# State space stage of a decoder kernel: x sigmoid(x) taken as h + h tanh(h), with one more scalar pass and GpSimd products

## The chip, the cores and the metric

One core of one Trainium2 chip runs the whole kernel. The metric is the device time of one execution in microseconds (us); the median of several executions stands for a kernel.

## What is computed

The kernel is a decoder of four layers over x of 64 x 64 x 128. The change is in one of its twelve stages, the state space layer of the third layer. Its reference, cut to what matters:

```python
xr = x @ w_in + b_in
xc, res = jnp.split(xr, 2, axis=-1)
u = jax.nn.silu(_causal_conv(xc, w_conv, b_conv))      # 4 taps along time
x_dbl = u @ w_x
dt, B, C = jnp.split(x_dbl, [DTR, DTR + N], axis=-1)   # N = 16
delta = jax.nn.softplus(dt @ w_dt)
deltaA = jnp.exp(delta[..., None] * A)
deltaBu = delta[..., None] * B[:, :, None, :] * u[..., None]
# h = a * h + bu along time, for each of the 16 states
y = jnp.einsum('bldn,bln->bld', hs, C) + u * D
return y * jax.nn.silu(res) @ w_out
```

silu(x) is x sigmoid(x). It is taken twice, of the convolved half (u) and of the gate half (res).

## The kernel before, in words

`state_space` (from line 2404) works on 8 groups of 512 positions (g = 0 to 7, `NG`), with the 256 inner channels in two halves of 128 partitions (c = 0, 1). Within a group it loops over the 16 states; step m = 16 g + k is state k of group g. Each engine has its own program in order, written out by hand, and they meet by semaphores.

Per step and half: the scalar engine makes the decay exp(A delta) (`decay`, L2697) into one of three PSUM banks in turn; GpSimd makes the product of du and the row of B (`inputs`, L2762) into one of two buffers per half; the vector engine runs the scan (`scan`, L2851) and multiplies by the row of C (`contribute`, L2859); TensorE lays out the row of C (`c_row`, L2527) and adds up over k (`accumulate`, L2544). I write scan(k,c) for the scan of state k, half c. The program of the vector engine in step k is scan(k,0), contribute(k-1,1), scan(k,1), contribute(k,0). In step k the scalar engine makes decay(k+1,0) and decay(k+1,1), and GpSimd the inputs of k+1. decay(k,c) may start when the scan three before it in order is done, since there are three banks; an input of k may start when the scan of k-2 in the same half is done.

Into these steps is woven the preparation of the next group, g+1. On the scalar engine: `raw` (L2627) takes the convolution out of PSUM with its bias in k = 1 and 3 (it waits for TensorE's four-tap convolution, L2501) and the gate half in k = 5 and 6 (L2491); in k = 6, behind those, `silu_u` (L2636) and `silu_res` (L2643), each one pass of 128 x 1024 with the Silu table; in k = 7 `copy_dt` and `copy_bc` (L2649, L2657) of the projection by w_x (`projected`, L2510), in k = 8 `high_part` (L2666), for which the vector engine waits in `below_high` (L2836) in k = 9, between contribute(8,1) and scan(9,1); in k = 9 and 10 `step_size` (L2674, L2675, and an Exp, L2681), in k = 11 `softplus` (L2685, Ln). On the vector engine in k = 7: layer norm statistics of group g+2 (L660, L666) and `residual` of group g-1 (L2869), after which TensorE may reuse the bank for `projected`. On GpSimd: `gated` (L2777, the product with the gate of the group before) in k = 2 and 3, a reciprocal root in k = 8, splitting of B and C in k = 9 to 11, `step_size` and `stepped_input` (L2767, L2772) in k = 12 to 15. SyncE fetches the rows of B by DMA, four steps ahead.

Group 0 has no group before it under which to hide, so its preparation (the head of the stage) is one chain through the engines.

The scalar engine holds one set of function tables at a time; where a pass needs another, the compiled program has an ACT_TABLE_LOAD ahead of it, shown with the line of that pass.

Of the kernel before, what the change touches and what calls it, by code (L numbers as in the profile page):

```python
# [18 lines left out]
ALU = mybir.AluOpType  # L19
ACT = mybir.ActivationFunctionType  # L20
# [6 lines left out]
GT = NT * P  # L27
# [612 lines left out]
NG = 8  # L640
# [1763 lines left out]
def state_space(nc, e, W):  # L2404
# [6 lines left out]
    use = ssm_order()  # L2411
    names = PN_SEMS + ("zeroed misc_mm misc_cp taps_done u_done res_done hi_done parts_own bc_parts relu_done sp_own sp_done "
                       "nb_raw nb_done dl_done du_done c_mm a_done bu_done hs_done hc_done acc_mm yo_done yr_done "
                       "h_mm h_cp raw_done low_done b_out b_in0 b_in1 b_in2 b_in3")
    with block_of(nc, "state_space", names) as (block, s):
        room = Room(e.arena)
        u_t = room.take(3 * 2 * GT)
# [17 lines left out]
        at, cbank, acc = (lambda i: e.bank((0, 1, 4)[i % 3])), (lambda m: e.bank(2 + m % 2)), (lambda c: e.bank(5 + c))  # L2435
        ln = PipedNorm(e, s, room, e.X, lambda g: xn, 1e-5)
        nb = room.pair(NT)

        @block.sync
        def _(sp):  # L2440
# [144 lines left out]
        def _(a):  # L2585
# [6 lines left out]
            def told(g):  # L2592
                return s["misc_cp"] if g else s["h_cp"]
# [22 lines left out]
            def raw(step, g):  # L2616
                c = int(step[-1]) % 2
                have(step, g)
                if step[0] == "c":
                    if g >= 1:  # L2620
                        a.wait_ge(s["u_done"], 2 * g)
                    out, bias = raw_u[:, c * GT:(c + 1) * GT], W("b_conv")[:, c:c + 1]
                else:
                    if g >= 2:
                        a.wait_ge(s["yr_done"], 2 * (g - 1))
                    out, bias = res(g, c), W("b_in")[:, 2 + c:3 + c]
                a.activation(out, bank(step, g), ACT.Identity, bias=bias).then_inc(told(g), 1)  # L2627

            def silu_u(g):
                if g == 0:  # L2630
                    a.wait_ge(s["h_cp"], HEAD["cv1"] + 1)
                else:
                    a.wait_ge(s["misc_cp"], use["cv1", g] + 1)
                if g >= 3:
                    a.wait_ge(s["misc_mm"], use["y", g - 3] + 1)
                a.activation(u_b(g), raw_u, ACT.Silu).then_inc(s["u_done"], 2)  # L2636

            def silu_res(g):
                if g == 0:
                    a.wait_ge(s["h_cp"], HEAD["m3"] + 1)  # L2640
                else:
                    a.wait_ge(s["misc_cp"], use["m3", g] + 1)
                a.activation(res_b(g), res_b(g), ACT.Silu).then_inc(s["res_done"], 1)  # L2643

            def copy_dt(g):
                have("db", g)
# [75 lines left out]
            for m in range(M):  # L2722
                g, k = m // N, m % N
                decay(m + 1, 0)
                decay(m + 1, 1)
                if g + 1 < NG:
                    if k in (1, 3):
                        raw(("cv0", "cv1")[k // 2], g + 1)
                    if k in (5, 6):
                        raw(("m2", "m3")[k - 5], g + 1)  # L2730
                    if k == 6:
                        silu_u(g + 1)
                        silu_res(g + 1)
                    if k == 7:
                        copy_dt(g + 1)
                        copy_bc(g + 1)
                    if k == 8:
                        high_part(g + 1)
                    if k in (9, 10):
                        step_size(k - 9, g + 1)  # L2740
                    if k == 11:
                        softplus(g + 1)
                if g + 2 < NG:
                    if k == 12:
                        scale(g + 2)
                    if k == 13:
                        copy_ln(g + 2)
                    if k in (14, 15):
                        channels(k - 14, g + 2)

        @block.gpsimd
        def _(q):
# [16 lines left out]
            def stepped_input(g, c):  # L2769
                q.wait_ge(s["dl_done"], 2 * g + c + 1)  # L2770
                q.wait_ge(s["u_done"], 2 * (g + 1))
                q.tensor_tensor(du(g, c), delta(g, c), u(g, c), ALU.mult).then_inc(s["du_done"], 1)  # L2772

            def gated(g, c):
                q.wait_ge(s["res_done"], g + 1)
                q.wait_ge(s["yo_done"], 2 * g + c + 1)
                q.tensor_tensor(u(g, c), u(g, c), res(g, c), ALU.mult).then_inc(s["yr_done"], 1)  # L2777

# [26 lines left out]
            for m in range(M):  # L2805
# [4 lines left out]
                inputs(m + 1)  # L2810
                if k in (2, 3) and g >= 1:
                    gated(g - 1, k - 2)
                if g + 1 < NG:
                    if k == 9:
                        middle(g + 1, "bu_done", 2 * (m + 2))
# [15 lines left out]
        def _(v):  # L2831
            def below_high(g):
                v.wait_ge(s["hi_done"], g + 1)
                if g >= 1:
                    v.wait_ge(s["bc_parts"], g)
                v.tensor_tensor(rest, raw_bc, bcp(g)[0:32, :], ALU.subtract).then_inc(s["low_done"], 1)  # L2836

            def first_step_size():
                v.wait_ge(s["relu_done"], 2)
# [31 lines left out]
            for i in range(3):  # L2871
                v.memset(tiles(at(i), NB)[:, :, 0:1], 0.0)
            v.memset(xp_all, 0.0).then_inc(s["zeroed"], 1)
            ln.stats(v, 0)
            ln.stats(v, 1)
            for c in range(2):
                for i in range(4):
                    ins = v.tensor_scalar(taps(c, i), e.ident, W("w_conv")[:, 4 * c + i:4 * c + i + 1], None, ALU.mult)
            ins.then_inc(s["taps_done"], 1)
            below_high(0)  # L2880
            first_step_size()
            for m in range(M):
# [1096 lines left out]
```

## Time and profile before

| | |
|---|---|
| median of 3 executions | 3262.33 us (3258.98 to 3262.79) |
| profiled execution, device time | 3257.66 us |
| profiled execution, span of the trace | 3255.9 us |
| state space stage in the trace | about 1490 to 2036 us |
| busy over the span | PE 82%, PEld 58%, DVE 59%, ACT 39%, POOL 44% |

PE is TensorE's matmuls and PEld its weight loads, DVE the vector engine, ACT the scalar engine, POOL GpSimd, SP SyncE. Lines such as L2851 are lines of the kernel before. An idle time with "<-" behind it was ended by what stands there. Where work of several engines overlaps, the time of the stage is set by the engine that never waits, and only what makes that one wait costs time.

### The profile page before, as it was taken

How to read it: one execution, taken by the hardware profiler on the slowest of the kernel's cores; microseconds unless marked ns; L12 is line 12 of the kernel's file. 1: busy time of each engine (PE TensorE's matmuls, PEld its weight loads, DVE VectorE, ACT ScalarE, POOL GpSimd, SP SyncE). 2: the span in 40 equal slices, each digit the busy share in tenths (PEclk: the TensorE clock that was granted, in tenths of full speed). 3: DMA queues.
4: the chain of work that ended last, by engine and by line, in shares of the span. 5: the costliest groups of instructions: out<-in, count | busy, mean ns of one | idle time of the engine just before them, and what ended most of it. 6: DMA issues, size and time to landing. Idle time of an engine off the chain costs nothing. (4 is left out here: it accounts for less than half of the span.)

```text
span 3255.9 us, 72437 instructions
## 1 busy us (share of the span) xinstructions
PE 2659.4 (82%) x28079; PEld 1876.5 (58%) x28079; DVE 1921.4 (59%) x4181; ACT 1277.8 (39%) x2160; POOL 1429.6 (44%) x1573
## 2 busy tenths in 40 slices
PE   7988849989999898885888886866769999982493
PEld 4655539967777565572333332534449898862493
DVE  4757752146777466533999999345657666544123
ACT  3533434411111144123666563432326656640253
POOL 5646532231222263543888877433541111115555
PEclk9989959989999899796999999877779999995797
DMA  7000016600000100152212221000000000001375
GB/s 243 2 1 2 2 49 176 171 29 3 3 3 3 42 15 8 41 168 67 69 66 70 71 66 52 1 1 1 2 8 9 5 9 5 2 2 56 112 229 156
DMA packets 116739, 164.30 MB, mean 50 GB/s; under 512 B 33264, under 2 KB 78704, under 8 KB 115952
## 3 DMA queue, kind: packets, MB, share of 16 engines
q1 hardware_dynamic: 101456, 143.13, 14.5%
q0 software_dynamic: 7168, 14.78, 1.3%
q8 instruction: 226, 3.70, 0.5%
q10 hardware_dynamic: 7776, 1.77, 0.3%
q14 instruction: 113, 0.93, 0.1%
HBM read 137.20 MB, written 25.62 MB: 50 GB/s over the span
## 5 line engine op out<-in xcount | busy, mean ns | idle before, releaser
L674 POOL TENSOR_SCALAR arena<-arena 128x4 f32<-128x4 f32 x120 | 27.6, 230 | 950.9 <-DVE arena L666 700.4
L2762 POOL TENSOR_TENSOR arena<-arena 128x512 f32<-128x512 f32 x256 | 321.3, 1271 | 71.4 <-DVE arena L2851 62.7
L2851 DVE TENSOR_TENSOR_SCAN arena<-ps,arena 128x512 f32<-128x512 f32 x256 | 313.0, 1223 | 31.3 <-ACT ps L2697 28.7
L2544 PE MATMUL ps<-arena,const_w 128*128 128x512 f32 x512 | 275.4, 623 | 16.8 <-DVE arena L2859 15.6
L163 PEld LDWEIGHTS ps<-L_attn_w,arena 128*128 128x128 f32 x1984 | 241.5, 193 | 59.6 <-issue 38.9
L163 PE MATMUL ps<-L_attn_w,arena 128*128 128x128 f32 x1984 | 258.8, 281 | 11.9 <-ACT arena L2627 4.7
L2697 ACT ACTIVATE ps<-arena,aneg 128x504 f32<-128x504 f32 x256 | 166.5, 677 | 61.6 <-DVE arena L2851 60.9
L1827 PE MATMUL ps<-arena,L_attn_w 128*128 128x512 f32 x384 | 184.5, 617 | 0.9 <-ACT arena L755 0.9
L1895 ACT ACTIVATE arena<-ps,L_attn_w 128x512 f32<-128x512 f32 x64 | 44.0, 687 | 332.7 <-PE ps L1827 332.7
L2859 DVE TENSOR_TENSOR arena<-arena,ps 128x512 f32<-128x512 f32 x256 | 170.8, 668 | 0.0
L435 ACT ACTIVATE arena<-ps 128x1024 f32<-128x1024 f32 x96 | 98.4, 1025 | 151.0 <-PE ps L337 151.0
L2544 PEld LDWEIGHTS ps<-arena,const_w 128*128 128x128 f32 x512 | 93.8, 195 | 106.8 <-DVE arena L2859 68.4
L429 ACT ACTIVATE arena<-arena 128x1024 f32<-128x1024 f32 x96 | 101.3, 1055 | 100.1 <-DVE arena L562 100.0
L491 POOL TENSOR_TENSOR arena<-arena,const_w 128x1024 f32<-128x1024 f32 x64 | 121.0, 1898 | 43.3 <-PE ps L325 35.9
L2291 DVE TENSOR_REDUCE arena<-arena 128x8 f32<-128x512 f32 x128 | 87.2, 681 | 84.1 <-ACT arena L2178 83.9
L163 PE MATMUL ps<-L_attn_w,ct_all 128*128 128x128 f32 x1024 | 131.0, 280 | 2.1 <-DVE arena L2307 2.0
L1125 DVE SCALAR_TENSOR_TENSOR arena<-ps,arena 128x64 f32 x108 | 30.7, 284 | 170.0 <-PE ps L925 160.7
L676 POOL TENSOR_TENSOR arena<-arena,mhalf 128x4 f32<-128x4 f32 x120 | 125.2, 1044 | 10.0
L700 POOL TENSOR_SCALAR arena<-x_all,arena 128x128 f32<-128x128 f32 x160 | 125.3, 796 | 7.4 <-POOL arena L676 6.4
L163 PEld LDWEIGHTS ps<-L_attn_w,ct_all 128*128 128x128 f32 x1024 | 123.0, 194 | 8.8 <-DVE arena L2307 3.8
L351 PEld LDWEIGHTS ps<-arena 128*64 128x64 f32 x3072 | 100.1, 139 | 42.0 <-issue 20.7
L337 PE MATMUL ps<-const_w,arena 128*128 128x128 f32 x768 | 105.9, 282 | 21.3 <-ACT arena L429 21.3
(460 smaller groups left out, 6389.8 us busy)
## 6 DMA issues: line engine op xcount, KB each, us to landing
arena<-b_rows SPq DMA_DIRECT2D x128, 256.0 KB, 3.1
arena<-zone_w SPq DMA_DIRECT2D x54, 512.0 KB
arena<-pair_w SPq DMA_DIRECT2D x40, 578.0 KB
arena<-rt SPq DMA_DIRECT2D x24, 384.0 KB
pair_in<-pair_free SPq DMA_DIRECT2D x1, 5200.0 KB, 37.8
arena<-pair_in SPq DMA_DIRECT2D x40, 130.0 KB
arena<-ctx SPq DMA_DIRECT2D x16, 256.0 KB, 3.5
arena<-pair_out SPq DMA_DIRECT2D x16, 256.0 KB, 5.2
```

What stands on the lines that cost most here:

```text
L163: ins = pe.matmul(out, src[:, j * P:(j + 1) * P], w, start=(i == 0), stop=(bias is None and i == len(chunks) - 1))
L337: ins = pe.transpose(e.bank(0, 2)[:, hp * P:(hp + 1) * P], sc(i)[:, hp * P:(hp + 1) * P], e.ident)
L429: a.activation(sc(i), sc(i), ACT.Exp, scale=scale).then_inc(s["p_ready"], 1)
L491: p_.tensor_tensor(kbd(i), repeat(k(g)[:, j * P:(j + 1) * P], HH), spread(e.hmask8, P), ALU.mult).then_inc(s["kbd_done"], 1)
L676: q.tensor_tensor(rs[:, NT:2 * NT], rs[:, 0:NT], self.e.mhalf[:, 0:NT], ALU.pow).then_inc(self.rstd_s, 1)
L700: q.tensor_scalar(self.dst(g)[:, j * self.step:j * self.step + D], self.src(g)[:, j * D:(j + 1) * D], mv[:, 2 * j:2 * j + 1], rs[:, NT + j ...
L1827: pe.matmul(e.bank(i), W(w)[:, col], xnT(g), start=True, stop=True).then_inc(s["qkg_mm"], 1)
L2544: pe.matmul(acc(c), e.ident, hc(m, c), start=(k == 0), stop=(k == N - 1)).then_inc(s["acc_mm"], 1)
L2697: a.activation(tiles(at(i), NB)[:, :, 1:S], tiles(delta(g, c), NB)[:, :, 1:S], ACT.Exp, scale=e.aneg[:, c * N + k:c * N + k + 1]).then_inc ...
L2762: q.tensor_tensor(bu(m, c), du(g, c), bs(m), ALU.mult).then_inc(s["bu_done"], 1)
L2851: v.tensor_tensor_scan(hs(m, c), at(2 * m + c), bu(m, c), 0.0, ALU.mult, ALU.add).then_inc(s["hs_done"], 1)
L2859: v.tensor_tensor(hc(m, c), hs(m, c), cbank(m), ALU.mult).then_inc(s["hc_done"], 1)
```

## The change

silu(x) = h + h tanh(h) with h = x/2. `raw` stores h in place of x (scale 0.5 and halved biases `half_b`, made by two small vector instructions in the head). `silu_u` becomes a Tanh pass and moves from k = 6 to k = 3, behind the `raw` of the second convolved half; the new `one_more` adds 1 to it in k = 4, behind the two decays; GpSimd multiplies by h in k = 4 and 5, one half in each. `silu_res` becomes a Tanh pass into a new tile `gate_t` and moves to k = 8, ahead of `high_part`; its `one_more` stands in k = 14, and GpSimd multiplies in k = 6 and 7 of the next group. In group 0 the vector engine does (tanh + 1) h for both in one instruction each (`first_silu`).

```diff
@@ ACT, raw @@
-                    out, bias = raw_u[:, c * GT:(c + 1) * GT], W("b_conv")[:, c:c + 1]
+                    out, bias = raw_u[:, c * GT:(c + 1) * GT], half_b[:, c:c + 1]
-                    out, bias = res(g, c), W("b_in")[:, 2 + c:3 + c]
-                a.activation(out, bank(step, g), ACT.Identity, bias=bias).then_inc(told(g), 1)
+                    out, bias = res(g, c), half_b[:, 2 + c:3 + c]
+                if g == 0:
+                    a.wait_ge(s["half_done"], 1)
+                a.activation(out, bank(step, g), ACT.Identity, bias=bias, scale=0.5).then_inc(told(g), 1)
@@ ACT, silu_u and silu_res @@
-                a.activation(u_b(g), raw_u, ACT.Silu).then_inc(s["u_done"], 2)
+                a.activation(u_b(g), raw_u, ACT.Tanh).then_inc(s["tu_done"], 1)
-                a.activation(res_b(g), res_b(g), ACT.Silu).then_inc(s["res_done"], 1)
+                if g >= 1:
+                    a.wait_ge(s["res_done"], 2 * g)
+                a.activation(gate_t, res_b(g), ACT.Tanh).then_inc(s["tr_done"], 1)
+
+            def one_more(t, sem, g):
+                a.wait_ge(s[sem], 2 * g)
+                a.activation(t, t, ACT.Identity, bias=1.0).then_inc(s[sem], 1)
@@ ACT, the loop over m, for the group g + 1 @@
-                    if k == 6:
+                    if k == 3:
                         silu_u(g + 1)
+                    if k == 4:
+                        one_more(u_b(g + 1), "tu_done", g + 1)
+                    if k == 8:
                         silu_res(g + 1)
+                    if k == 14:
+                        one_more(gate_t, "tr_done", g + 1)
@@ POOL @@
+            def silu_u(g, c):
+                q.wait_ge(s["tu_done"], 2 * g + 1)
+                q.tensor_tensor(u(g, c), u(g, c), raw_u[:, c * GT:(c + 1) * GT], ALU.mult).then_inc(s["u_done"], 1)
+
+            def silu_res(g, c):
+                q.wait_ge(s["tr_done"], 2 * g + 1)
+                q.tensor_tensor(res(g, c), gate_t[:, c * GT:(c + 1) * GT], res(g, c), ALU.mult).then_inc(s["res_done"], 1)
+
             def gated(g, c):
-                q.wait_ge(s["res_done"], g + 1)
+                q.wait_ge(s["res_done"], 2 * g + c + 1)
@@ POOL, the loop over m, behind inputs(m + 1) @@
+                if k in (4, 5) and g + 1 < NG:
+                    silu_u(g + 1, k - 4)
+                if k in (6, 7) and g >= 1:
+                    silu_res(g, k - 6)
@@ DVE, the head @@
+            def first_silu():
+                v.wait_ge(s["tu_done"], 1)
+                v.scalar_tensor_tensor(out=u_b(0), in0=u_b(0), scalar=1.0, in1=raw_u, op0=ALU.add,
+                                       op1=ALU.mult).then_inc(s["u_done"], 2)
+                v.wait_ge(s["tr_done"], 1)
+                v.scalar_tensor_tensor(out=res_b(0), in0=gate_t, scalar=1.0, in1=res_b(0), op0=ALU.add,
+                                       op1=ALU.mult).then_inc(s["res_done"], 2)
+            for i, part in enumerate((W("b_conv"), W("b_in")[:, 2:4])):
+                ins = v.tensor_scalar(half_b[:, 2 * i:2 * i + 2], part, 0.5, None, ALU.mult)
+            ins.then_inc(s["half_done"], 1)
```

## Rows read from the trace of the kernel before

**Rows 1.** Busy time by window; columns: window, its us, each engine, PEclk, DMA share, GB/s
```profile
1650.00:1710.00 60.00, 49.88 (x130) 19.91 (x130) 58.39 (x76) 37.23 (x57) 50.09 (x45) 1.00 0.21 67
```
**Rows 2.** Groups of ACT, 1490 to 2050: count, busy us, mean ns, idle before
```profile
L2697 ACT ACT_TABLE_LOAD x15 | 19.2, 1283 | 1.7 <-DVE arena L2841 1.4
...
L2636 ACT ACT_TABLE_LOAD x7 | 9.0, 1283 | 0.1
```
**Rows 3.** Groups of DVE, 1490 to 2050
```profile
L2851 DVE TENSOR_TENSOR_SCAN arena<-ps,arena 128x512 f32<-128x512 f32 x256 | 313.0, 1223 | 31.3 <-ACT ps L2697 28.7 <-POOL arena L2762 1.5
```
**Rows 4.** Timeline of DVE: start, us, what, [idle before it], three scans behind Silu
```profile
1567.84 1.22 DVE L2851 TENSOR_TENSOR_SCAN arena<-ps,arena 128x512 f32<-128x512 f32 x1 [1.98 <-ACT ps L2697]
...
1630.28 1.22 DVE L2851 TENSOR_TENSOR_SCAN arena<-ps,arena 128x512 f32<-128x512 f32 x1 [1.40 <-ACT ps L2697]
...
1940.11 1.22 DVE L2851 TENSOR_TENSOR_SCAN arena<-ps,arena 128x512 f32<-128x512 f32 x1 [2.51 <-ACT ps L2697]
```
**Rows 5.** Timeline, steps 4 to 7 of group 1
```profile
1612.21 3.74 POOL L2762 TENSOR_TENSOR arena<-arena 128x512 f32<-128x512 f32 x3
...
1615.29 0.69 ACT L2627 ACTIVATE arena<-ps,L_attn_w 128x512 f32<-128x512 f32 x1 [3.46 <-PE ps L2501]
...
1615.87 1.89 ACT L2697 ACTIVATE ps<-arena,aneg 128x504 f32<-128x504 f32 x3
...
1616.74 1.22 DVE L2851 TENSOR_TENSOR_SCAN arena<-ps,arena 128x512 f32<-128x512 f32 x1
...
1620.16 1.22 DVE L2851 TENSOR_TENSOR_SCAN arena<-ps,arena 128x512 f32<-128x512 f32 x1
...
1623.58 1.23 DVE L2851 TENSOR_TENSOR_SCAN arena<-ps,arena 128x512 f32<-128x512 f32 x1
```
**Rows 6.** Timeline, step 5 of group 0
```profile
1553.59 2.65 ACT L2697 ACTIVATE ps<-arena,aneg 128x504 f32<-128x504 f32 x4
...
1554.30 1.22 DVE L2851 TENSOR_TENSOR_SCAN arena<-ps,arena 128x512 f32<-128x512 f32 x1 [0.37 <-ACT ps L2697]
```
**Rows 7.** Timeline, steps 7 to 9 of group 1
```profile
1628.21 0.66 DVE L2869 TENSOR_TENSOR x_all<-ps,x_all 128x512 f32<-128x512 f32 x1
...
1628.93 1.96 PE L2510 MATMUL ps<-arena,L_attn_w 128*96 128x512 f32 x4
...
1630.92 0.59 ACT L2649 ACTIVATE arena<-ps 64x512 f32<-64x512 f32 x1
...
1632.02 1.26 ACT L2697 ACTIVATE ps<-arena,aneg 128x504 f32<-128x504 f32 x2
...
1633.31 0.63 ACT L2666 ACTIVATE bcp<-arena 32x512 bf16<-32x512 f32 x1
...
1633.71 1.22 DVE L2851 TENSOR_TENSOR_SCAN arena<-ps,arena 128x512 f32<-128x512 f32 x1
...
1635.54 0.68 DVE L2836 TENSOR_TENSOR arena<-arena,bcp 32x512 f32<-32x512 f32 x1
```
**Rows 8.** Groups of POOL, 1490 to 2050
```profile
L2777 POOL TENSOR_TENSOR arena<-arena 128x512 f32<-128x512 f32 x16 | 20.3, 1271 | 8.2 <-DVE arena L2864 8.2
```
**Rows 9.** Timeline of the head
```profile
1505.02 1.06 ACT L2643 ACTIVATE arena<-arena 128x1024 f32<-128x1024 f32 x1
1507.73 0.69 ACT L2627 ACTIVATE arena<-ps,L_attn_w 128x512 f32<-128x512 f32 x1 [1.66 <-PE ps L2501]
...
1521.81 1.28 ACT L2681 ACT_TABLE_LOAD   x1
...
1526.66 1.22 DVE L2841 TENSOR_TENSOR arena<-arena 128x1024 f32<-128x1024 f32 x1 [7.84 <-ACT arena L2685]
```
**Rows 10.** Groups of DVE, 1490 to 2050: a vector instruction of few columns
```profile
L3141 DVE TENSOR_SCALAR arena<-L_xattn_w 128x1 f32<-128x1 f32 x1 | 0.2, 156 | 1.0 <-PEq L55 1.0
```
**Rows 11.** Groups of ACT, 2050 to 2170, the next stage (Tanh L3062, Exp L3040)
```profile
L3062 ACT ACTIVATE arena<-ps,arena 128x512 f32<-128x512 f32 x8 | 5.5, 687 | 19.1 <-PE ps L2987 19.1
L3040 ACT ACTIVATE arena<-arena 128x512 f32<-128x512 f32 x8 | 5.0, 620 | 0.0
```

More of the change, by code:

```diff
@@ L2413, in state_space @@
                        "nb_raw nb_done dl_done du_done c_mm a_done bu_done hs_done hc_done acc_mm yo_done yr_done "
-                       "h_mm h_cp raw_done low_done b_out b_in0 b_in1 b_in2 b_in3")
+                       "h_mm h_cp raw_done low_done tu_done tr_done half_done b_out b_in0 b_in1 b_in2 b_in3")
     with block_of(nc, "state_space", names) as (block, s):
@@ L2437, in state_space @@
         nb = room.pair(NT)
+        gate_t, half_b = room.take(2 * GT), room.take(4)
         @block.sync
@@ L2879, in _ @@
             ins.then_inc(s["taps_done"], 1)
+            first_silu()
             below_high(0)
```

## The prediction

> **What bounds the kernel now.** The page gives no answer for this stage, so I read in this order: busy time by window, groups by line, the vector engine in order of time, then one group of all engines. By window the stage belongs to the vector engine: 58.4 of 60 us, against 50.1 on GpSimd, 49.9 on TensorE and 37.2 on the scalar engine [rows 1]. Its scans wait 28.7 us for decays of the scalar engine and 1.5 us for GpSimd [rows 3]; nothing else holds it up between its head and its end. So a microsecond in which the scan waits is a microsecond of the kernel, and everything else lies under the scans. The reader is to see that GpSimd has 10 us of slack in 60, and that the slack is worth only what the order of its program lets it use.
>
> In order of time one scan starts 1.71 us after the last (1616.74 to 1620.16 is two) [rows 5]. Behind the Silu passes of each group it sits idle: 1.98 us in group 0, 1.40 in groups 1 to 5 (five alike, one shown), 2.51 in group 6 [rows 4]. Normally a successor overlaps the end of its forerunner by 0.09 us (a raw of 0.69 at 1615.29, the next at 1615.87, is 0.58 apart and overlaps 0.11), so counted from start to start the losses are 2.07, 1.49 and 2.60.
>
> **Removed: the table changes.** Seven loads stand ahead of Silu and seven of the fifteen at the decays are its way back, 14 x 1.283 = 18.0 us of scalar time [rows 2]. In the next stage eight Exp and eight Tanh passes alternate without any load [rows 11], so the two functions share a set, and I take it that Tanh among decays needs none. What goes on the path is only the scan's waits: 2.07 + 5 x 1.49 + 2.60 = 12.1 us. A gain of the full 18.0 isn't to be had, since the scan never waited for that much. The Trainium skill (ScalarE: Activation LUTs, What ACT_TABLE_LOAD costs) puts a switch to another set at 2.66 us, drain included, which would make 37 us of scalar time. The row has the load alone, 1.283 us with 0.1 idle ahead of it over seven, so the trace does not show the drain.
>
> **Added first: Tanh in k = 3.** TensorE hands over the second convolution late: the raw pass starts at 1615.29 after 3.46 us of waiting, decay(5,0) follows at 1615.87 and ends at about 1616.56, and scan(5,0) starts at 1616.74 [rows 5]. There is 0.14 us of room. Tanh must wait for the end of raw (1615.98), starts at about 1616.05, lasts 1.06 as other 128 x 1024 passes do [rows 9], and decay(5,0) can start 0.96 later, 1617.01, ends 1617.69, and the scan starts at 1617.73 instead of 1616.74: +0.99. In group 0 the decay has no room at all (decay 1553.59, scan 1554.30 after a wait of 0.37 [rows 6]); there it is 1553.01 + 0.69 + 0.07 + 0.96, decay from 1554.7, scan at 1555.44: +1.14.
>
> **Added second: GpSimd's wait for one_more.** This is the dear one. In k = 4 GpSimd has ended inputs(5) at about 1615 (three from 1612.21, the third of which is already the first of k = 6 [rows 5]); now silu_u(0) stands ahead of that third one and waits for one_more. one_more follows decay(5,0) and decay(5,1): 1617.64 + 0.63 = 1618.27, done 1619.33. Queued behind this wait are the inputs of k = 6. GpSimd's products come every 1.25 us (3.74 for three) [rows 5] and last 1.27 [rows 8]. silu_u(0) at 1619.40, input (6,0) at 1620.65, done 1621.92. scan(6,0) is due at 1620.16 + 0.99 = 1621.15 and starts at 1621.95: +0.80. Input (6,1), silu_u(1), input (7,0) follow at 1621.90, 1623.15, 1624.40, done 1625.67. scan(7,0) is due at 1623.58 + 1.79 = 1625.37, starts 1625.70: +0.33. After that the statistics and residual of k = 7 give GpSimd room for silu_res (2.5 us in k = 6 and 7). Sum here 2.12 in groups 1 to 6, 2.27 in group 0.
>
> **Added third: the gate's Tanh ahead of high_part.** With the stall behind Silu gone, the next late thing is the projection. TensorE can't start it before residual is done (1628.87), starts 1628.93, and copy_dt starts at 1630.92 [rows 7]. Decay(9,0) follows 1.10 later, 1632.02, ends 1632.70. scan(8,0) would be due at 1628.79, scan(9,0) at 1632.22, and starts at 1632.74: +0.52. Until now this hid in the Silu stall. Then decay(9,1), and Tanh in front of high_part: high_part ends 0.63 + 0.63 + 0.96 + 0.63 = 2.85 after decay(9,0) starts, 2.90 with its signal. below_high was due 1.83 after scan(9,0) (1633.71 to 1635.54 [rows 7]), that is 0.72 + 1.83 = 2.55 after decay(9,0): +0.35. In group 0 there is no residual and nothing of this; in group 6 no statistics cover it (about 1.2 us less vector work in k = 7), part of which TensorE's order takes, so I put 1.1 for 0.52.
>
> **Added where it costs nothing:** one_more in k = 14 (the scalar engine waits for TensorE there), silu_res on GpSimd in k = 6 and 7, the other decays, and SyncE's rows of B, fetched four steps ahead. If the cover of silu_res were gone, each group would pay up to 2.5 us more.
>
> **The head.** Its Tanh of the gate may need a load of 1.28, which with the pass ends at 1507.4, ahead of the next raw at 1507.73: hidden. The load ahead of the first Exp (1521.81, on the chain) then goes, -1.28. The projection now waits for first_silu, priced by a 128 x 1024 product of two SBUF tiles, 1.22 [rows 9], plus 0.05 of signal: +1.27; as a fused form it may take 1.5. Two instructions of few columns ahead of the statistics, between 0 and 0.156 each [rows 10]: +0.2. Head: +0.2, between -0.2 and, if the first Exp keeps its load, +1.8.
>
> **The sum.** Group 0: 2.27 - 2.07 = +0.20. Groups 1 to 5: 2.12 + 0.52 + 0.35 - 1.49 = +1.50 each, +7.5. Group 6: 2.12 + 1.1 + 0.35 - 2.60 = +0.97. Head +0.2. Total +8.9: 3257.7 of the profiled execution becomes 3266.6. That one is 4.7 below the median, so beside the median 3262.3 I say 3271.2. Bounds: the terms at their smallest (0.9, 0.6, 0.1, 0, 0.1) leave +0.2 a group and +1 in all; at their largest (1.1, 0.9, 0.4, 0.7, 0.5) +2.1 a group, with the head's upper end +16. So 3263 to 3278 for this case.
>
> **The rivals.** (1) *Faster: the waits are gone and nothing takes their place.* That holds if raw comes 0.99 us earlier at k = 3, the point from which Tanh fits ahead of decay(5,0), and one_more with it and 0.8 earlier still, so that input (6,0) is ready in time. Then -12.1 + 0.2: 3250.4. For it: 10 us of slack on GpSimd, 23 on the scalar engine [rows 1]. Against: 0.14 us of room at 1616.74, in every group. The Trainium skill's rule (ScalarE: Activation LUTs, Table sets: the hidden batching unit) to batch passes by set rather than by function speaks for this rival. Chance 0.13. (2) *Only the scalar terms count, GpSimd's are covered:* its wait for one_more costs the scans nothing if inputs (6,0) is not late. 0.99 + 0.52 + 0.35 - 1.49 = +0.37 a group, some +2.5 in all, 3265. This asks for one_more 0.8 us sooner against the scans than I have it, as if GpSimd needed no 0.07 to start and one_more didn't stand behind decay(5,1). Against: both stand in the code. Chance 0.22. (3) *The tables aren't shared in this stage:* then each Tanh brings two loads, 5.1 us a group on decays with no room, 7 x 5.1 + 9 = +45: 3307. Against it [rows 11]. Chance 0.04. (4) GpSimd falls further behind than I have it, so that its root and splitting in k = 8 to 11 come late too: up to 2 us a group more, 3285. Chance 0.06. Forecast 0.55.
>
> **How the numbers follow.** About 0.2%, 6.5 us, is what a measurement of this kernel tells from no change, so same is 3255.8 to 3268.8. Slower: 0.48 of the forecast's 0.55, 0.02 of case 2, cases 3 and 4: 0.58. Same: the rest of the forecast, most of case 2 and 0.01 of case 1: 0.28. Faster 0.14. The range leaves out most of case 1 and all of 3 and 4's far part: 3257 to 3281.
>
> **What would show it.** ACT loads fall from 31 in the stage to 17; Those at L2697 are eight, behind Ln, and L2636 has none. The wait of scans for the Tanh'd decays appears at scan(5,0) as 0.9 us, for POOL at scan(6,0) and (7,0) as 0.7 and 0.25, for ACT at scan(9,0), and below_high waits 0.3. GpSimd sits 4.7 us ahead of silu_u(0) in each group. If scans wait for POOL nowhere, my second term is wrong; if scan(5,0) doesn't wait, the first; if loads remain at L2697 beyond those behind Ln, case 3.

## The result, and the profile after

| | before | after |
|---|---|---|
| median of 7 runs each, us | 3262.3 (3258.53 to 3262.95) | 3273.19 (3271.89 to 3290.77) |
| ratio of the two, 95% interval | | 1.0047 (1.003 to 1.0064) |
| profiled execution, its own time, us | 3257.7 | 3290.77 |
| its span, us | 3255.9 | 3289.0 |
| state space stage in the trace, us | 544.58 | 561.90 |
| stage start to first scan, us | 40.68 | 42.77 |
| scan(5,0) of one group to that of the next, groups 1 to 5, us | 61.97 | 63.76 (65.5 and 65.8 in two of them) |
| ACT table loads in the stage | 31 | 17 |

The change costs 10.9 us at the medians; 8.9 was predicted. 14.5 us of what the profiled execution of after takes more lie ahead of the stage (it begins at 1504.62 and not at 1490.07), where nothing was changed, so I compare the stage and not the spans.

The groups of the scalar engine and of the vector engine in the stage, 1480 to 2060 (columns as in [rows 2]: count, busy us, mean ns, idle before and what ended it), answer to [rows 2] and [rows 3]:

```profile
L2694 ACT ACT_TABLE_LOAD x8 | 10.3, 1283 | 0.1
L2706 ACT ACT_TABLE_LOAD x8 | 10.3, 1283 | 1.6 <-DVE arena L2875 1.4
L2690 ACT ACT_TABLE_LOAD x1 | 1.3, 1283 | 0.0
...
L2885 DVE TENSOR_TENSOR_SCAN arena<-ps,arena 128x512 f32<-128x512 f32 x256 | 313.2, 1223 | 39.7 <-ACT ps L2706 31.3 <-issue 6.1 <-POOL arena L2776 1.5
L2862 DVE TENSOR_TENSOR arena<-arena,bcp 32x512 f32<-32x512 f32 x8 | 7.6, 950 | 7.8 <-ACT bcp L2675 7.8
L2790 POOL TENSOR_TENSOR arena<-arena 128x512 f32<-128x512 f32 x14 | 17.8, 1268 | 33.5 <-ACT arena L2652 33.5
```

The 14 loads around Silu are gone. The scans last what they did, 1223 ns, and wait longer: 39.7 us where it was 31.3, though the seven stalls behind Silu, 12 us of it, should have left. below_high (L2862) has become 950 ns long, where the one of [rows 7] took 0.68 us. GpSimd waits 33.5 us ahead of the 14 products of silu_u, which is 4.8 a group.

Steps 3 to 9 of group 1 in order of time (start, us, what, idle before it), against [rows 5] and [rows 7]:

```profile
1633.38 0.69 ACT L2630 ACTIVATE arena<-ps,arena 128x512 f32<-128x512 f32 x1 [3.46 <-PE ps L2502]
1634.10 1.06 ACT L2639 ACTIVATE arena<-arena 128x1024 f32<-128x1024 f32 x1
1635.06 1.27 ACT L2706 ACTIVATE ps<-arena,aneg 128x504 f32<-128x504 f32 x2
1635.76 1.22 DVE L2885 TENSOR_TENSOR_SCAN arena<-ps,arena 128x512 f32<-128x512 f32 x1 [0.84 <-ACT ps L2706]
1636.27 1.04 ACT L2652 ACTIVATE arena<-arena 128x1024 f32<-128x1024 f32 x1
1637.39 1.27 POOL L2790 TENSOR_TENSOR arena<-arena 128x512 f32<-128x512 f32 x1 [4.61 <-ACT arena L2652]
1638.62 2.50 POOL L2776 TENSOR_TENSOR arena<-arena 128x512 f32<-128x512 f32 x2
1639.97 1.22 DVE L2885 TENSOR_TENSOR_SCAN arena<-ps,arena 128x512 f32<-128x512 f32 x1 [0.70 <-issue]
...
1643.66 1.22 DVE L2885 TENSOR_TENSOR_SCAN arena<-ps,arena 128x512 f32<-128x512 f32 x1 [0.17 <-issue]
...
1652.79 1.22 DVE L2885 TENSOR_TENSOR_SCAN arena<-ps,arena 128x512 f32<-128x512 f32 x1 [0.42 <-ACT ps L2706]
1653.38 1.06 ACT L2648 ACTIVATE arena<-arena 128x1024 f32<-128x1024 f32 x1
1654.28 2.94 POOL L2776 TENSOR_TENSOR arena<-arena 128x512 f32<-128x512 f32 x2
1654.47 0.63 ACT L2675 ACTIVATE bcp<-arena 32x512 bf16<-32x512 f32 x1
1655.13 0.97 DVE L2862 TENSOR_TENSOR arena<-arena,bcp 32x512 f32<-32x512 f32 x1 [0.54 <-ACT bcp L2675]
```

The reader can walk the whole prediction here. raw ends, Tanh (L2639) runs, the decay starts behind it, and scan(5,0) is late. one_more (L2652) comes behind both decays, GpSimd's silu_u (L2790) behind it, and the first of the two inputs (L2776, 1.27 long) ends at 1639.88, just ahead of scan(6,0) at 1639.97: the profile calls that wait "issue", but the times name GpSimd. Then the gate's Tanh (L2648) stands in front of high_part (L2675), and below_high waits 0.54.

In numbers, from the start of one scan to that of the next, less the pitch of 1.71, in groups 1 to 5 (before, after): scan(5,0) 0 and 0.93; (6,0) 0 and 0.79; (7,0) 0 and 0.26; (8,0) 3.27 and 1.77; (9,0) 0 and 0.50; (9,1) 0.83 and 1.63. All five groups agree within 0.02, but for 0.16 more at (5,0) in one.

One thing was not on the list. In groups 3 and 4 scan(12,0), which is 0.20 late everywhere else, comes 1.78 and 2.21 late. The timeline of after shows the step sizes' matmuls and the copy behind them, in group 2 and then in group 3, with the late scan:

```profile
1724.71 1.12 PE L2518 MATMUL ps<-arena,L_attn_w 64*128 64x512 f32 x2
1725.87 0.60 ACT L2683 ACTIVATE arena<-ps 128x512 f32<-128x512 f32 x1 [2.33 <-PE ps L2518]
...
1789.10 2.07 PE L2518 MATMUL ps<-arena,L_attn_w 64*128 64x512 f32 x2
1791.20 0.60 ACT L2683 ACTIVATE arena<-ps 128x512 f32<-128x512 f32 x1 [3.91 <-POOL arena L2776]
...
1793.98 1.22 DVE L2885 TENSOR_TENSOR_SCAN arena<-ps,arena 128x512 f32<-128x512 f32 x1 [1.70 <-ACT ps L2706]
```

and the windows around them (columns as in [rows 1]):

```profile
1784.00:1787.00 3.00, 1.66 (x4) 0.30 (x2) 3.00 (x4) 2.05 (x4) 2.79 (x4) 1.00 0.27 74
1787.00:1790.00 3.00, 2.70 (x4) 0.91 (x5) 3.00 (x5) 0.29 (x1) 2.84 (x4) 0.63 0.10 36
1790.00:1793.00 3.00, 3.00 (x5) 0.69 (x4) 2.29 (x3) 1.76 (x3) 2.94 (x3) 0.50 0.20 66
```

TensorE's granted clock goes from 1.00 to 0.50, that is from 2.4 to 1.2 GHz, for 6.8 us here and 10.2 in group 4. The step sizes' matmuls (L2518) take 2.07 us instead of 1.12 and start late; they end at 1791.17, just ahead of the copy, though its row names GpSimd. So the copy starts 65.33 behind that of group 2 where the period is 63.76: 1.57 late, and Exp, the decay and the scan with it. In the same place of before (1639 to 1642) the granted clock is 1.00. Before has low stretches too, of which those at the end of a group matter here: 3.4 us in groups 2 to 5, behind which no scan is late, and 6.8 us in group 0, behind which the first scan of group 1 is 0.46 late.

### The profile page after: what moved, and what is told of

It is laid out like the page before. It is cut to its first block and busy times, and to the rows that moved or that the text cites. A ratio compares the mean times of both kernels' runs of the same rounds, so it can differ in the third digit from the quotient of the medians.

```text
span 3289.0 us, 72479 instructions
## 1 busy us (share of the span) xinstructions
PE 2669.9 (81%) x28079; PEld 1886.6 (57%) x28079; DVE 1926.7 (59%) x4185; ACT 1272.1 (39%) x2160; POOL 1465.1 (45%) x1601
## 3 DMA queue, kind: packets, MB, share of 16 engines
q10 hardware_dynamic: 7776, 1.77, 0.3%
## 5 line engine op out<-in xcount | busy, mean ns | idle before, releaser
L2776 POOL TENSOR_TENSOR arena<-arena 128x512 f32<-128x512 f32 x256 | 321.9, 1279 | 33.4 <-DVE arena L2885 24.2
L2885 DVE TENSOR_TENSOR_SCAN arena<-ps,arena 128x512 f32<-128x512 f32 x256 | 313.2, 1223 | 39.7 <-ACT ps L2706 31.3
L2706 ACT ACTIVATE ps<-arena,aneg 128x504 f32<-128x504 f32 x256 | 166.9, 675 | 59.6 <-DVE arena L2885 58.0
L435 ACT ACTIVATE arena<-ps 128x1024 f32<-128x1024 f32 x96 | 98.3, 1024 | 156.7 <-PE ps L337 156.7
```

Source lines behind the costliest of these rows:

```text
L2706: a.activation(tiles(at(i), NB)[:, :, 1:S], tiles(delta(g, c), NB)[:, :, 1:S], ACT.Exp, scale=e.aneg[:, c * N + k:c * N + k + 1]).then_inc ...
L2776: q.tensor_tensor(bu(m, c), du(g, c), bs(m), ALU.mult).then_inc(s["bu_done"], 1)
L2885: v.tensor_tensor_scan(hs(m, c), at(2 * m + c), bu(m, c), 0.0, ALU.mult, ALU.add).then_inc(s["hs_done"], 1)
```

## The experiments

Two theories stood against each other at first. *Order:* the cost is made of waits at the named scans, each from the place of an instruction in its queue. *Volume:* the change gives GpSimd 28 more products and the scalar engine 14 more passes, and the engines are slower for it wherever the work stands. Each ratio below is against before on the same chip, whose medians were 3261.7, 3260.5 and 3261.22.

**The changed kernel again.** No edit.

> The changed kernel once more, for a trace that is not lengthened ahead of the stage. Order theory (what costs is where the new passes and products stand in the programs of the scalar engine and GpSimd): one group takes 63.75 us against 61.97 before, made of scan(5,0) +0.93, scan(6,0) +0.79, scan(7,0) +0.26, scan(9,0) +0.50, below_high and scan(9,1) +0.80, less 1.49; the head is 2.1 us longer; total 10 to 12 us over before. Volume theory (the added 28 products on GpSimd and their contention with the vector engine cost, wherever they stand): the same times, but vector instructions longer than before throughout, by 1% or more.

3277.09 us (10 runs, 3266.36 to 3284.62), ratio 1.0046 (1.0032 to 1.006). The waits at the scans are those of after within 0.03, but for 0.34 less at (3,0) of group 0 and 0.15 at (5,0) of two groups, and the low clock is in groups 3 and 4 again (+1.6, +2.0). The volume theory wanted vector instructions longer by 1% throughout. Against loads_only, which ran on the same chip without the new work, they are not: scans 1215 ns and 1214, contribute 658 and 659. Longer are only below_high, 957 ns and 683, and the GpSimd products beside it, by which the mean of the inputs is 1286 and 1271 ns.

**The loads alone.** Before, with Tanh in Silu's place; the product with x is left out, so only the loads differ from before.

```diff
-                a.activation(u_b(g), raw_u, ACT.Silu).then_inc(s["u_done"], 2)
+                a.activation(u_b(g), raw_u, ACT.Tanh).then_inc(s["u_done"], 2)
-                a.activation(res_b(g), res_b(g), ACT.Silu).then_inc(s["res_done"], 1)
+                a.activation(res_b(g), res_b(g), ACT.Tanh).then_inc(s["res_done"], 1)
```

> The kernel before with Tanh in place of Silu in the same two passes of every group, so the product with x is left out: this is the change of tables alone. Order theory: the 14 loads go, the scan's wait behind them goes (1.49 us a group from start to start), and the next late thing is the projection, +0.5 at scan(9,0): 61.0 us a group, some 7 us under before, head unchanged. If the loads' whole time counted it would be 18 us under before; if the scan waited for the two passes and not for the loads, no change.

3253.27 us (10 runs, 3249.61 to 3258.08), ratio 0.9976 (0.9966 to 0.9986): with nothing else moved, the loads are worth 8.4 us and not 18. scan(8,0) comes 1.50 earlier, as predicted (1.49), and scan(9,0) is at once 0.50 late: the projection, which the Silu stall had covered. A third part was not expected: each of groups 1 to 5 ends with a stretch of 6.8 us at 1.2 GHz, and the first scan of the next group is 0.41 to 0.47 late. The period is 61.4: 61.97 - 1.50 + 0.50 + 0.44. Between this kernel and after_again, on the same chip, lie 23.8 us. That is the price of the new work where it stands.

**GpSimd's products one step later.**

```diff
-                if k in (4, 5) and g + 1 < NG:
-                    silu_u(g + 1, k - 4)
+                if k in (5, 6) and g + 1 < NG:
+                    silu_u(g + 1, k - 5)
```

> The changed kernel with the two products of silu_u on GpSimd one step later (k = 5 and 6), nothing else moved. Order theory: inputs of k = 6 no longer stand behind the wait for one_more, so scan(6,0) and scan(7,0) wait no more, 1.05 us a group less than the changed kernel: 62.7 us a group, 3264 to 3267 in all. Volume theory: the same products, the same time as the changed kernel, 63.75 us a group.

3267.92 us (10 runs, 3263.3 to 3272.95), ratio 1.0021 (1.0009 to 1.0032). The waits at scan(6,0) and (7,0) are gone, both from one edit that moves no work off any engine. It brings 9.2 us of the 15.4: 7 x 1.05 = 7.4 for the waits, and 1.6 for below_high, 0.68 of it in group 0. Two groups have the low clock here as well. The period is 62.52. It is 1.24 shorter than 63.76, 1.05 of it the two waits and 0.18 a shorter below_high (scan(9,1) 1.45 late instead of 1.63), for which I had no reason yet.

**Tanh behind the decays too.** In addition to the last, Tanh in k = 4, and one_more in k = 5 ahead of the raw pass.

```diff
-                    if k == 3:
-                        silu_u(g + 1)
                     if k == 4:
+                        silu_u(g + 1)
+                    if k == 5:
                         one_more(u_b(g + 1), "tu_done", g + 1)
```

> As the last, and on the scalar engine the Tanh of u moves from k = 3 (behind raw) to k = 4 (behind decay(5,0) and decay(5,1)), one_more to k = 5 ahead of raw. Order theory: scan(5,0) waits no more either, 0.93 us less again: 61.8 us a group, about 3258 to 3261 in all, the level of before. Left are +0.50 at scan(9,0) and +0.80 at below_high. Volume theory: no change against the changed kernel.

A miss: 3273.68 us (9 runs, eight of them 3263.93 to 3278.51 and one 4402.27), ratio 1.0032 (1.0018 to 1.0046), not faster than pool_later. The wait at scan(5,0) went, as expected. Two things came in its place. below_high takes 1.56 us (1.72 in one group), in tanh_k4's own timeline:

```profile
1707.45 2.94 POOL L2776 TENSOR_TENSOR arena<-arena 128x512 f32<-128x512 f32 x2
1707.71 1.56 DVE L2862 TENSOR_TENSOR arena<-arena,bcp 32x512 f32<-32x512 f32 x1 [0.54 <-ACT bcp L2675]
```

and four groups have a stretch of 7 to 10 us at the low clock, each with 2.1 to 2.2 us at scan(12,0). So there were two unknown terms, and I formed a theory for each. *Exclusion:* below_high, with two SBUF inputs, can't start while a GpSimd product runs, so its length is set by where that product stands. *Idle TensorE:* the moved passes open a gap in TensorE's work, behind which the clock falls.

**The gate's Tanh behind high_part.** If the Tanh in front of high_part is what costs, the period falls; by the exclusion theory it does not, since below_high only meets the product earlier in its life.

```diff
                     if k == 8:
-                        silu_res(g + 1)
...
                         high_part(g + 1)
+                        silu_res(g + 1)
```

> The changed kernel with the gate's Tanh (silu_res) behind high_part instead of ahead of it in k = 8. By the prediction's own step alone: below_high is no longer held, the 0.54 us wait goes, scan(9,1) is 0.8 us less late, 63.0 us a group. By the contention theory (a vector instruction with two SBUF inputs runs longer while GpSimd multiplies): the wait goes, but below_high now lies wholly beside GpSimd's inputs of k = 10 and lasts about 1.56 us instead of 0.98, so a group stays near 63.7 us and the total near that of the changed kernel.

3276.43 us (7 runs, 3266.2 to 3283.17), ratio 1.0046 (1.0031 to 1.0061), a period of 63.77 against 63.76. The wait of below_high went, and its length took all of it back:

```profile
1707.21 2.94 POOL L2775 TENSOR_TENSOR arena<-arena 128x512 f32<-128x512 f32 x2
1707.54 1.50 DVE L2861 TENSOR_TENSOR arena<-arena,bcp 32x512 f32<-32x512 f32 x1
```

**A product in before.** To make exclusion in the kernel that does not have it: two 128 x 512 products of GpSimd in k = 9, ahead of the middle of the norm.

```diff
+                        for c in range(2):
+                            q.tensor_tensor(extra[:, c * GT:(c + 1) * GT], u(g, 0), u(g, 1), ALU.mult).then_inc(s["extra_own"], 1)
+                        q.wait_ge(s["extra_own"], 2 * (g + 1))
```

> The kernel before with two more 128x512 products on GpSimd (two SBUF inputs each, into a tile that nobody reads) in k = 9 of groups 0 to 6, ahead of middle, so that they lie beside below_high. Contention theory: below_high, 0.68 us in every group before, takes about 1.5 us, and a group 0.8 us more than 61.97. If GpSimd and the vector engine don't hinder each other, below_high stays at 0.68 and the group at 61.97, since GpSimd has that much slack.

3259.77 us (10 runs, 3255.51 to 3265.52), ratio 0.9998 (0.9988 to 1.0008). A miss in size: below_high took 0.80 and not 1.5.

```profile
1635.48 2.94 POOL L2817 TENSOR_TENSOR arena<-arena 128x512 f32<-128x512 f32 x2
1636.50 0.80 DVE L2840 TENSOR_TENSOR arena<-arena,bcp 32x512 f32<-32x512 f32 x1
```

Its first product began at 1635.48 and ended, 1.27 later, at 1636.75, only 0.25 behind the start of below_high. That made the theory exact: the length is 0.68, its length alone, plus the rest of the GpSimd instruction under way, less about 0.13. For this one 0.68 + 0.25 - 0.13 = 0.80. For tanh_k4, whose product ends at 1708.72, it is 0.68 + 1.01 - 0.13 = 1.56; for gate_behind 0.68 + 0.94 - 0.13 = 1.49. And the pair of products lasts 2.94 where a pair alone lasts 2.50: the second is held until below_high is done. These were fitted to what had been seen. The next two were written down ahead.

**Two aligned probes.** A small product (128 x 128) first, so that the large one begins where below_high will meet it in its middle; then the same with a copy, which has one SBUF input.

```diff
+                        q.tensor_tensor(extra[:, 0:P], u(g, 0)[:, 0:P], u(g, 1)[:, 0:P], ALU.mult).then_inc(s["extra_own"], 1)
+                        q.tensor_tensor(extra[:, GT:2 * GT], u(g, 0), u(g, 1), ALU.mult).then_inc(s["extra_own"], 1)
```

> The kernel before with a 128x128 and a 128x512 product on GpSimd in k = 9 ahead of middle, into a tile nobody reads, so aligned that below_high starts early in the larger one. Exclusion theory: the larger starts some 0.6 us ahead of below_high and has 0.6 to 0.8 left, so below_high takes 1.15 to 1.35 us in every group. A theory by which both only share bandwidth in proportion gives 0.8 as in probe_product.

> As probe_product2 with a 128x1024 copy (one SBUF input) on GpSimd in place of the 128x512 product. If the exclusion belongs to GpSimd's two-input products, below_high stays at 0.68; if it belongs to any GpSimd instruction, below_high waits for the whole rest of the copy, to 1.2 us or more.

One execution each (3265.88 and 3261.22 us). below_high takes 1.21 to 1.22 in all groups with the product and 0.96 to 0.97 with the copy. probe_product2 in order of time:

```profile
1642.05 1.27 POOL L2817 TENSOR_TENSOR arena<-arena 128x512 f32<-128x512 f32 x1
1642.65 1.21 DVE L2840 TENSOR_TENSOR arena<-arena,bcp 32x512 f32<-32x512 f32 x1
```

and probe_copy2:

```profile
1639.60 1.04 POOL L2817 COPY arena<-arena 128x1024 f32<-128x1024 f32 x1
1640.21 0.97 DVE L2840 TENSOR_TENSOR arena<-arena,bcp 32x512 f32<-32x512 f32 x1
```

The rule gives 0.68 + 0.67 - 0.13 = 1.22 and 0.68 + 0.43 - 0.13 = 0.98. So a copy holds the vector engine up as a product does; the 1.2 us expected beside it was too much, since only 0.43 us of the copy were left.

The rule was not made for one row of each kernel. In all fourteen traces below_high runs 112 times: 41 times with no GpSimd instruction under way, 0.68 each, and 71 times, in eleven kernels, with one; these took 0.78 to 1.72, and the rule gives each within 0.01.

**The head with Silu.** Group 0 keeps Silu and its biases; the halved biases for the other groups are made later.

```diff
-                if g == 0:
+                if g == 1 and step == "cv0":
                     a.wait_ge(s["half_done"], 1)
...
+                if g == 0:
+                    a.activation(u_b(0), raw_u, ACT.Silu).then_inc(s["u_done"], 2)
+                    return
```

> The changed kernel with group 0 as in the kernel before (Silu passes by the table that is loaded there anyway, no first_silu, the halved biases made later). Expected: the head is 2.05 us shorter than the changed kernel's at the same granted clock (about 40.7 or 36.7 us to the first scan against 42.8 or 38.8), the groups stay at 63.75 us, total 2 us under the changed kernel, which timing alone can hardly tell.

3273.58 us (6 runs, 3270.12 to 3277.16), ratio 1.0038 (1.0026 to 1.0051). The head takes 37.50 where after_again has 38.79. They lie between the end of the u pass and copy_dt, 3.39 us in after_again and 2.05 here, so they are first_silu. I had expected 36.7, which is what loads_only has (36.75). The 0.75 that stay lie ahead of the u pass, among matmuls at the low clock, which lasts until 12.4 us into this head and 10.9 into that of loads_only. In after_again it lasts until 12.3, and the u pass is 0.72 later than in loads_only: as much as here, where no halving instruction stands ahead of it.

**Everything moved.** The head as before, Tanh in k = 4, silu_u's products in k = 5 and 6, copy_dt and copy_bc in k = 8 behind the decays, the gate's Tanh in k = 9, silu_res on GpSimd in k = 0 and 1.

```diff
-                    if k == 7:
+                    if k == 8:
                         copy_dt(g + 1)
                         copy_bc(g + 1)
...
-                if k in (6, 7) and g >= 1:
-                    silu_res(g, k - 6)
+                if k in (0, 1) and g >= 1:
+                    silu_res(g, k)
```

> All moves together: head as before; Tanh of u in k = 4, one_more in k = 5 ahead of raw, its products on GpSimd in k = 5 and 6; copy_dt and copy_bc behind the decays of k = 8; the gate's Tanh in k = 9; silu_res on GpSimd in k = 0 and 1. Order theory: no wait at scan(5,0), (6,0), (7,0), (9,0): 61.97 - 1.49 = 60.5 us a group, plus what below_high grows by beside GpSimd (0.3 to 0.9): 60.8 to 61.4 us, some 4 to 8 us under before, 3254 to 3258. Volume theory: as slow as the changed kernel, 63.75 us. If a low TensorE clock falls into k = 10 to 12 of a group, that group is 1.6 to 2.2 us longer at scan(12,0).

3253.39 us (10 runs, 3248.77 to 3257.91), ratio 0.9975 (0.9965 to 0.9985). No scan from (5,0) to (9,0) waits for any new instruction; the period is 61.15 in four groups, 63.18 in one that has the low clock. below_high still takes 1.37:

```profile
1699.08 2.50 POOL L2784 TENSOR_TENSOR arena<-arena 128x512 f32<-128x512 f32 x2
1700.76 1.37 DVE L2870 TENSOR_TENSOR arena<-arena,bcp 32x512 f32<-32x512 f32 x1
```

The second product starts 1.25 behind the first and ends at about 1701.60: 0.68 + 0.84 - 0.13 = 1.39.

**The norm's root later.** GpSimd's 1/sqrt and offset stand in k = 8, ahead of the inputs that below_high meets. All of the last, and this:

```diff
-                if k == 8 and g + 2 < NG:
+                if k == 11 and g + 2 < NG:
```

> all_moved with the reciprocal root on GpSimd (L674 to L686, 1.95 us) in k = 11 behind lowest instead of k = 8. Exclusion theory (a vector instruction with two SBUF inputs waits for the end of the GpSimd product under way, its time is 0.68 us plus what is left of that product less 0.13): GpSimd has then ended the inputs of k = 10 before below_high starts, so below_high takes 0.68 us again instead of 1.37, and a group 60.45 us instead of 61.15; total 4 to 5 us under all_moved, 3248 to 3250. If the 1.37 us had another cause, 61.15 us a group as before.

3251.49 us (11 runs, 3242.94 to 3257.47), ratio 0.9971 (0.9959 to 0.9982): 9.7 us faster than before and 20 or more faster than the changed kernel. below_high is 0.68 in every group and the period 60.62 to 60.95; no group has the low clock at scan(12,0). The 0.17 to 0.5 above the 60.45 expected lie at the first scan of the next group. It beats both kernels; that it beats all_moved too, by 4 to 5 us as expected, the times don't show (0.9971 and 0.9975, with intervals that overlap).

**TensorE kept at work.** tanh_k4, with the row of C in k = 9 and 10 computed three times, the same result each time.

```diff
+                    if m // N < NG - 1 and m % N in (9, 10):
+                        for _ in range(2):
+                            row_of(cbank(m), m // N, N + m % N)
```

> tanh_k4 with TensorE kept busier where it idles: the row of C for k = 9 and 10 is computed three times instead of once (the same result each time) in groups 0 to 6. Clock theory: the stretches of low granted clock of 7 to 11 us in k = 9 to 12, four of them in tanh_k4, each with 2.1 to 2.2 us at scan(12,0), become rare, since TensorE no longer idles ahead of them; total 5 to 8 us under tanh_k4, 3265 to 3268. If what TensorE does ahead has no part in it, the stretches stay and the total is that of tanh_k4 or slower.

3267.39 us (9 runs, 3263.92 to 3272.62), ratio 1.0025 (1.0015 to 1.0034). That is 6.3 us under tanh_k4, but on another chip, and the interval overlaps with that of tanh_k4 (1.0018 to 1.0046). Between the one trace of each, groups with the low clock ahead of scan(12,0) go from four to two, and the first to the last scan takes 497.9 us instead of 502.1. Group 1 in tanh_k4, by windows and with its scan(12,0):

```profile
1643.00:1646.00 3.00, 2.24 (x5) 0.63 (x5) 2.62 (x2) 2.32 (x5) 2.92 (x3) 1.00 0.10 36
1646.00:1649.00 3.00, 1.53 (x4) 0.64 (x5) 3.00 (x5) 1.62 (x3) 2.79 (x5) 0.81 0.25 87
1649.00:1652.00 3.00, 3.00 (x5) 0.81 (x3) 3.00 (x5) 0.00 (x0) 2.84 (x3) 0.50 0.23 61
...
1655.71 1.22 DVE L2885 TENSOR_TENSOR_SCAN arena<-ps,arena 128x512 f32<-128x512 f32 x1 [2.12 <-ACT ps L2706]
```

The first two windows again, in tensor_fed:

```profile
1643.00:1646.00 3.00, 2.09 (x5) 0.71 (x5) 3.00 (x5) 1.48 (x3) 2.86 (x4) 1.00 0.25 87
1646.00:1649.00 3.00, 2.92 (x7) 1.00 (x7) 3.00 (x5) 1.60 (x3) 2.84 (x4) 1.00 0.29 86
```

In the traces the kernel with more matmuls on TensorE has the shorter stage. With one trace of each, and the number of such groups one or two in kernels that differ as little as gate_behind and after, that the repeated matmuls did it is likely and not shown. What picks the groups stays open too: in group 2 of after TensorE is busy for 1.60 of the 3 us (1720.3 to 1723.3) that answer to the first window of group 3 shown above with 1.66, and there the clock did not fall.

## Why the prediction was right, and where its sizes were not

The sign and the mechanism were right: the load goes from the path once a group, and new waits larger than it come. Step by step, in groups 1 to 5:

| step of the prediction | predicted | measured |
|---|---|---|
| Silu stall removed, at scan(8,0) | -1.49 | -1.50 |
| Tanh ahead of decay(5,0) | +0.99 | +0.93 |
| GpSimd behind one_more, scan(6,0) | +0.80 | +0.79 |
| the same, scan(7,0) | +0.33 | +0.26 |
| projection uncovered, scan(9,0) | +0.52 | +0.50 |
| high_part behind the gate's Tanh | +0.35 | +0.80 (0.51 wait, 0.29 length of below_high) |
| a group | +1.50 | +1.79 |

**Removed.** Right in count, 17 loads and none ahead of Silu's place, and in worth. The cap of 12.1 us was right too; loads_only has less, since the projection takes 0.50 back at once while its copies stand in k = 7; all_moved, with the copies in k = 8, has no such wait. **GpSimd's term** was the contested one, and with it rival 2, which had it covered. pool_later removes these two waits, 7.4 of the 9.2 us that it gives, so it is not covered. **Rival 1** did not come, but all_moved and root_later show what it needs: places in which none of the new instructions stands in front of a decay or of an input. Rivals 3 and 4 fell: no load at L2706 but the eight behind Ln, and no scan of k = 8 to 11 waits for an input of GpSimd.

**below_high** is the term of the sum that was mis-sized: 0.80 and not 0.35. The wait was foreseen, at 0.35, and came to 0.51 from start to start. The length was not: I took it as 0.68 from [rows 7], and it became 0.97, since below_high, pushed back, meets a product that it had passed ahead of. The Trainium skill (SBUF — State Buffer, Who interferes with whom) says that a vector instruction with two SBUF inputs contends with a GpSimd instruction that reads SBUF, that the shared port pair is an exclusive lock, and that issue order decides who blocks. The traces agree: in all 71 places below_high, 0.68 alone, waits for the GpSimd instruction that was there first, growing to between 0.78 and 1.72, and a product that comes behind it is held in turn. I had the row's length and did not ask what was running beside it.

**The head** was mis-sized in the same direction: +2.05 (42.77 against 40.68, and 38.79 against loads_only's 36.75) where I put +0.2, and above even the +1.8 that I gave as its upper end. The step that failed here is "the load ahead of the first Exp then goes". In after's head, scalar and vector engine:

```profile
1519.81 1.06 ACT L2648 ACTIVATE arena<-arena 128x1024 f32<-128x1024 f32 x1
...
1526.67 1.06 ACT L2639 ACTIVATE arena<-arena 128x1024 f32<-128x1024 f32 x1
1527.85 1.22 DVE L2866 SCALAR_TENSOR_TENSOR arena<-arena 128x1024 f32<-128x1024 f32 x1 [17.94 <-ACT arena L2639]
...
1538.45 1.28 ACT L2690 ACT_TABLE_LOAD   x1
```

Both Tanh passes ran without a load, on the set that was there. It had been loaded for a Silu: the last load ahead of the stage stands at the Silu pass of L1389, at 1331.00, and in before the two Silu passes of the head run on it. That set has Tanh and not Exp, so the load at Exp stays. first_silu (1.22 and its signal) costs 1.29 to 1.34, as sized (1.27). The rest, 0.7, differs between the two pairs. In after_again it lies ahead of the u pass; head_silu has it there too, without the halving instructions, so it goes with the low clock, which ended later in both than in loads_only, and not with the change. In after 0.2 lies ahead of the u pass and 0.6 behind it, where the projection's matmuls (L2511), now later and wholly at the low clock, take 3.73 us instead of 3.16. This head took 38.79 to 42.78 us in six traces and that of before 36.75 to 40.68 in five, so a pair of heads shows the change only as far as the clock fell alike in both. What is sure of it is first_silu, 1.3: the +0.2 of the sum lacks this because it took off the load that stayed.

**The low clock** was no term at all: +3.6 us in two groups of both profiled executions of this kernel. With it the account of after_again's stage is: group 0 +0.75, groups 1 to 5 +8.9, group 6 +1.05, head +2.05, scan(3,0) of group 0 +0.4, clock +3.6, less the 0.46 that before loses at the first scan of group 1, together +16.3. The stage is 557.05, and before's, with the head that loads_only shows (3.93 shorter), 540.65: +16.4. The medians moved by 10.9 (7 runs) and 15.4 (10 runs), whose own spread is larger than the difference. The 0.4 at scan(3,0) is not the change's: there loads_only, without the new work, is 1.19 late, after_again 0.88 and before 0.48. Without it and the clock, the terms that were predicted come to +12.8, against +8.9: 2.25 more from below_high in groups 1 to 5, 1.85 more from the head, 0.55 more in group 0, where below_high took 1.37 us and nothing was put for it, and 0.1 in group 6, less 0.8 for the small misses at scan(5,0), (6,0), (7,0) and (9,0).

That the range held is owed to its bounds and not to the sum: the two terms that I had wrong had the same sign, and a third was missing. The sum's 8.9 lies near the 10.9 of the medians by luck: the stage grew by 16 in after_again and 17 in after. There is a slip in the chances as well: by their own parts slower and faster come to 0.60 and 0.12, and not to 0.58 and 0.14.

## What to carry to other kernels

Where one engine sets the pace, a pass that is taken off its feeder is worth only the stall that it causes, here 1.50 of the 2.57 us of its loads, and a new instruction costs more by its place in the queue than by its length: two products of GpSimd moved by one step of the loop gave back 9.2 us. Before a freed queue is filled again, put each new instruction behind whatever the pacing engine waits for next. When an instruction moves by half a microsecond, look at what runs beside it at its new place: another engine may hold its ports there.

## What the runs showed of the hardware

- **A vector instruction with two SBUF inputs and a GpSimd instruction exclude each other.** below_high took 0.68 us alone (41 times) and 0.78 to 1.72 beside a GpSimd instruction (71 times), in each case 0.68 plus what was left of that instruction less 0.13, within 0.01; the next product was then held, 1.70 to 1.72 instead of 1.27 (40 times). The scans, with one input in PSUM and one in SBUF, lie beside such products all the time and are not longer for more of them (1215 ns and 1214). A copy with one input (128 x 1024, 1.04 us) does it as well: 0.97.
- **The set that is loaded for Silu holds Tanh and not Exp.** Two Tanh passes ran without a load in the head, and a load of 1.283 us stood at the Exp behind them. A load had at most 0.1 us of idle time over eight ahead of it.
- **TensorE's clock fell to 1.2 GHz for 7 to 10 us** in the middle of a group in six of the eleven other kernels and in the changed kernel, where TensorE had waited in part of the microseconds ahead; each time the next step size was late and scan(12,0) with it, 1.6 to 2.0 us more than else. At the end of a group, stretches of 3.4 us made no scan late in before, and behind those of 6.8 us the next scan was 0.4 to 0.5 late in before and in loads_only. With repeated matmuls in the gap two groups had it where four had it, in one trace of each. Which groups it takes is not settled.
